# Query, key and value products as three 16-bit products of halves, with the splitting work dealt anew to the engines

## The reference

```
mod = silu(c) @ wmod                      # sa, ca, ga, sb, cb, gb for each batch
h   = layernorm(x) * (1 + ca) + sa
q, k, v = split(h @ w_qkv)                # 256 -> 3 * 256, 16 heads of 16
q, k = elu(rope(q) * s) + 1, elu(rope(k) * s) + 1
out[t] = q[t] . sum(k v, up to t) / max(q[t] . sum(k, up to t), 1e-6)   # causal linear attention
x   = x + ga * (out @ w_out)
h   = layernorm(x) * (1 + cb) + sb
x   = x + gb * (mixture of 8 experts of width 1024, top 2 of a softmax router)(h)
```

## Time and profile before

| | us |
|---|---|
| median of 3 runs (779.16 to 779.76) | 779.57 |
| span of the profiled execution | 776.0 |
| busy in the span: PE / DVE / ACT / POOL | 714.8 / 628.2 / 571.2 / 518.5 |
| steady part of the first phase, one chunk | about 9.5 |

### The profile page before, as it was taken

One profiled execution on the slowest core, in us unless ns is written; L12 is line 12 of the kernel. 1 busy time (PEld: TensorE's weight loads), 2 busy tenths in 40 slices (PEclk: granted clock), 3 DMA queues, 4 the chain that ended last, 5 costly groups with the idle time before them and its releaser, 6 DMA issues.

```text
span 776.0 us, 24871 instructions
## 1 busy us (share of the span) xinstructions
PE 714.8 (92%) x8105; PEld 549.7 (71%) x8105; DVE 628.2 (81%) x1494; ACT 571.2 (74%) x1108; POOL 518.5 (67%) x535
## 2 busy tenths in 40 slices
PE   8799999999999999845799999999999999999994
PEld 5467777777777776634677777777777777777772
DVE  4999999999999888778577777777777777777773
ACT  2799899999999998740476767777776767677772
POOL 5777777777777776547466666666666666666642
PEclk9999999999999999855799999999999999999997
DMA  6324344444443412310343343344333333443410
GB/s 226 113 67 133 110 135 120 131 120 139 124 140 116 151 64 67 120 48 8 96 77 69 71 73 74 76 70 79 70 75 69 77 69 76 76 72 76 72 21 1
DMA packets 52854, 69.27 MB, mean 89 GB/s; under 512 B 8864, under 2 KB 44080, under 8 KB 52736
## 3 DMA queue, kind: packets, MB, share of 16 engines
q0 software_dynamic: 18176, 27.06, 18.6%
q1 hardware_dynamic: 34560, 40.61, 16.9%
HBM read 46.50 MB, written 22.05 MB: 88 GB/s over the span
## 4 chain that ended last, share of the span: by engine, by line
PE 51%; DVE 2%; POOL 2%; issue 1%; DMA 1%; ACT 0%; POOLq 0%; DVEq 0%; ACTq 0%
PE hidden L1457 16%; PE bank L1475 15%; PE hidden L1459 8%; PE bank L1477 8%; PE bank L1292 2%; POOL mod_b L960 1%; PE bank L1309 0%; DMA xt<-ffn_rows,gi 0%; DMA out_dram<-x,si 0%; DVE stage L651 0%; PE bank L1300 0%; PE bank L1389 0%; POOL out_dram L1008 0%; DVE feat L652 0%; POOL mod_b L962 0%
## 5 line engine op out<-in xcount | busy, mean ns | idle before, releaser
L1457 PE MATMUL hidden<-qstT,w1hi_k 128*128 128x256 f16 x1136 | 197.9, 274 | 0.7 <-DVE qstT L755 0.7
L1459 PE MATMUL hidden<-qstT,w1lo_k 128*128 128x128 f16 x1136 | 193.6, 220 | 0.0
L1475 PE MATMUL bank<-w,amhi 128*128 x568 | 188.4, 379 | 0.1
L1477 PE MATMUL bank<-w,amlo 128*128 x568 | 154.8, 273 | 0.0
L1008 POOL DMA_INDIRECT out_dram<-x,si x71 | 115.2, 1622 | 38.8 <-issue 25.8
L791 DVE TENSOR_TENSOR amlo<-am,amhi 128x512 f16<-128x512 f32 x142 | 98.3, 693 | 49.2 <-ACT am L1168 49.2
L1457 PEld LDWEIGHTS hidden<-qstT,w1hi_k 128*128 x1136 | 111.7, 98 | 14.0 <-issue 1.1
L1459 PEld LDWEIGHTS hidden<-qstT,w1lo_k 128*128 x1136 | 111.6, 98 | 0.2
L1309 PE MATMUL bank<-wq,hT 128*128 128x512 f32 (+1 forms) x256 | 98.8, 511 | 1.3 <-DVE hT L524 1.2
L1475 PEld LDWEIGHTS bank<-w,amhi 128*128 128x128 f16 x568 | 55.6, 98 | 59.9 <-issue 0.4
L1167 ACT ACTIVATE amhi<-am 128x512 f16<-128x512 f32 x142 | 88.1, 620 | 0.3 <-DVE am L785 0.3
(11 more groups left out here) (219 smaller groups left out, 1783.6 us busy)
## 6 DMA issues: line engine op xcount, KB each, us to landing
stage<-in_L_ffn_w_dram SPq DMA_DIRECT2D x32, 512.0 KB, 4.3
xt<-in_L_attn_x_dram SPq DMA_DIRECT2D x32, 128.0 KB, 4.0
out_dram<-x SPq DMA_DIRECT2D x32, 128.0 KB, 3.7
ffn_rows<-h SPq DMA_DIRECT2D x32, 128.0 KB, 1.8
ffn_rows<-am SPq DMA_DIRECT2D x32, 128.0 KB, 4.2
am<-mod_rows SPq DMA_DIRECT2D x16, 128.0 KB, 4.0
mod_b<-mod_rows SPq DMA_DIRECT2D x8, 256.0 KB, 4.4
w<-in_L_wmod_dram SPq DMA_DIRECT2D x6, 256.0 KB, 4.6
```

Of the source, the lines that this page charges most:

```text
L1457: t.matmul(dst.rearrange("p (q n) -> p q n", q=2), w1s[0][k][g][:, w_], both, start=(k == 0), stop=False)
L1459: last = t.matmul(dst[:, P:2 * P], w1s[1][k][g][:, w_], both[:, 0, :], start=False, stop=(k == KT - 1))
L1475: t.matmul(y[:, :], ghi[:, m.p, c_m], w2s[mt // 2][:, bass.ds(w_, 2 * D)], start=(mt == 0), stop=False)
L1477: last = t.matmul(y[:, D:2 * D], glo[:, m.p, c_m], w2s[mt // 2][:, bass.ds(w_, D)], start=False, stop=(mt == MT - 1))
```

## The change

- From chunk 3 on (`PLAIN = 3`) `qk` and `v` are three 16-bit products per contraction step (high x high, high x low, low x high). Chunks 0 to 2 still take the 32-bit products, straight from the staged weights `wq_raw`.
- New steps: `wqh` (ACT, twice 128 x 768, once) and `wql` (DVE, twice 128 x 768, once) split the weights, scaled by 64. `hh` (ACT, 128 x 256) and `hl` (POOL, 128 x 256) split `hT`. `hT` and `h16` have one buffer each, and `v` and `qk` wait for `hl`.
- `hTe` moves from DVE to ACT (`Identity` with scale and bias from tensors). `whi` moves from ACT to POOL (two `tensor_scalar`).
- `slo` becomes one POOL instruction of 128 x 512 for q and k together; the slots of low x low hold zeros.
- `vhi`, `vlo` and the first three `rope`s take a factor of 64 into account; instruction counts of `vlo` stay, `rope` of chunks 0 to 2 has three instructions, not two.
- All orders are new. On DVE `den`, `rec`, `at` (now lag 4) stand around `ve` and ahead of `nb`, and `f` follows `nb`. On POOL `rs` is followed by `whi`. The closing of DVE no longer ends with `wlo`.

```diff
-ORDER_DVE = (("st2", 5), ("st", 0), ("mv2", 5), ("mv", 0), ("ve", 0), ("f", 2), ("sl0", 3), ("nb", 0), ("rope", 1),
-             ("stl", 3), ("x1", 4), ("hTe", 0), ("sl1", 3), ("wlo", 1), ("vlo", 0), ("den", 3), ("rec", 3), ("at", 3))
-ORDER_POOL = (("rs", 0), ("shk", 2), ("slo", 2), ("wb", 4), ("R", 1), ("xm2", 5), ("h2", 5))
-ORDER_ACT = (("exp", 2), ("sh0", 3), ("shq", 2), ("sth", 3), ("aTe", 4), ("xn", 0), ("sh1", 3), ("whi", 1),
-             ("kTs", 2), ("xn2", 5), ("vhi", 0), ("h2Te", 6), ("qTs", 2), ("lge", 6))
+ORDER_PE = (("aT", 4), ("state", 3), ("ear", 3), ("hT", 0), ("sc1", 3), ("pj", 4), ("Tk", 2), ("h2T", 6), ("pv0", 3),
+    ("v", 0), ("Tq", 2), ("lg", 6), ("pv1", 3), ("sc0", 2), ("qk", 0))
+ORDER_DVE = (("st", 0), ("mv2", 5), ("mv", 0), ("den", 4), ("ve", 0), ("rec", 4), ("at", 4), ("nb", 0), ("f", 2),
+    ("sl0", 3), ("rope", 1), ("stl", 3), ("x1", 4), ("sl1", 3), ("wlo", 1), ("vlo", 0), ("st2", 4))
+ORDER_POOL = (("h2", 7), ("rs", 1), ("whi", 2), ("wb", 5), ("shk", 3), ("slo", 3), ("hl", 1), ("R", 2), ("xm2", 6))
+ORDER_ACT = (("lge", 7), ("exp", 2), ("sh0", 3), ("xn", 0), ("aTe", 4), ("shq", 2), ("sth", 3), ("hTe", 0),
+    ("hh", 0), ("sh1", 3), ("kTs", 2), ("xn2", 5), ("h2Te", 6), ("vhi", 0), ("qTs", 2))
-OPENING_PE = {0: (("hT", 0), ("qk", 0), ("v", 0)), 1: (("hT", 0), ("mod1", 0), ("v", 0), ("qk", 0))}
+OPENING_PE = {0: (("hT", 0), ("v", 0), ("qk", 0)),
+OPENING_ACT = {0: (("xn", 0), ("hh", 0), ("wqh", 0), ("hTe", 0)),
...
-                g.tensor_tensor(qst[:, :, 1:4:2, :], f[:, 0].broadcast_to([P, NH, 2, HD]), qst[:, :, 0:3:2, :],
-                                ALU.subtract)
-                g.tensor_tensor(kst[:, :, 2:4, :], f[:, 1].broadcast_to([P, NH, 2, HD]), kst[:, :, 0:2, :],
-                                ALU.subtract).then_inc(a_["slo"], 1)
+                g.tensor_tensor(lows, feat[:, :].rearrange("p (q h d) -> p q h d", q=2, h=NH), highs, ALU.subtract)\
+                    .then_inc(a_["slo"], 1)
+            def h_low16(m):
...
+                wait(pool, a_["hh"], m.n - PLAIN + 1)
+                g.tensor_tensor(h16[:, 1, :], hT[:, :], h16[:, 0, :], ALU.subtract).then_inc(a_["hl"], 1)
+            def weights_high(m):
+                wait(pool, s_w[m.p], 16 * (m.pairs + 1))
+                g.tensor_scalar(piece(m, 0, 0), staged(m, 0), WS, None, ALU.mult)
+                g.tensor_scalar(piece(m, 0, 1), staged(m, 1), WS, None, ALU.mult).then_inc(a_["whi"], 1)
...
+            def h_modulated(m):
...
+                for k in range(KT):
+                    last = v.activation(hT[:, k * P:(k + 1) * P], bank[0][:, k * P:(k + 1) * P], ACT.Identity,
+                                        bias=mod_t[:, bass.ds(k * B + m.b, 1)],
+                                        scale=mod_t[:, bass.ds((KT + k) * B + m.b, 1)])
...
+            def product16(dst, m, lo):
+
+                for k in range(KT):
+                    hi_, lo_ = (h16[:, c, k * P:(k + 1) * P] for c in range(2))
+                    last = mm3(dst, hi_, lo_, wq16[:, k, 0, lo], wq16[:, k, 1, lo], start=(k == 0), stop=(k == KT - 1))
+                return last
```

More of the change, by code:

```diff
@@ new lines @@
+OPENING_DVE = {0: (("st", 0), ("mv", 0), ("ve", 0), ("nb", 0)),
+    1: (("st", 0), ("mv", 0), ("ve", 0), ("nb", 0), ("vlo", 1), ("rope", 1), ("vlo", 0), ("wql", 1), ("wlo", 1)),
+    2: (("st", 0), ("sl1", 3), ("mv", 0), ("sl0", 3), ("ve", 0), ("stl", 3), ("nb", 0), ("rec", 3), ("mv2", 5), ("f", 2), ("rope", 1), ("x1", 4), ("wlo", 1), ("vlo", 0), ("at", 3), ("wql", 1), ("st2", 5), ("den", 3))}
+OPENING_ACT = {0: (("xn", 0), ("hh", 0), ("wqh", 0), ("hTe", 0)),
+    1: (("hh", 0), ("vhi", 1), ("xn", 0), ("hTe", 0), ("vhi", 0), ("rows", 0))}
@@ L222, in adaln_block @@
         v16 = sb("v16", [P, CPB, 2, NH, VW], F16)
-        qst = sb("qst", [P, NH, 4, HD], F16)
-        kst = sb("kst", [P, NH, 4, HD], F16)
+        stacks = sb("stacks", [P, 2 * STACK + 3 * HD], F16)
+        qst, kst = (stacks[:, q * STACK:(q + 1) * STACK].rearrange("p (h c d) -> p h c d", h=NH, c=4) for q in range(2))
+        by_stack = stacks[:, 0:2 * STACK].rearrange("p (q h c) -> p q h c", q=2, c=4 * HD)
+        highs, nothing = by_stack[:, :, :, 0:HD], by_stack[:, :, :, 3 * HD:4 * HD]
+        lows = stacks[:, HD:2 * STACK + 3 * HD].rearrange("p (q n) -> p q n", q=2)[:, :, 0:STACK].rearrange(
+            "p q (h c) -> p q h c", c=4 * HD)[:, :, :, 0:HD]
         qstT = sb("qstT", [P, 8 * P], F16)
@@ L293, in adaln_block @@
         wmod_raw = [[late(w2s[(k * 3 + j) // 4], (k * 3 + j) % 4 * 512, 512) for j in range(3)] for k in range(KT)]
+        wq_raw = [late(w1s[0][0][k], 0, 3 * D) for k in range(KT)]
         rw_raw = late(w2s[2], 1280, D, E)
@@ L514, in first_modulation @@
                     link(v.tensor_scalar(mod_t[:, n_], bank[1][:, n_], add, None, ALU.add))
-            def h_modulated(m):
-                wait(dve, a_["hT"], m.n + 1)
-                wait(dve, a_["qk"], m.n - 1)
-                wait(dve, a_["v"], m.n - 1)
-                if isinstance(m.n, int) and m.n == 0:
-                    first_modulation()
-                for k in range(KT):
-                    last = v.tensor_scalar(hT[:, m.p, k * P:(k + 1) * P], bank[0][:, k * P:(k + 1) * P],
-                                           mod_t[:, bass.ds((KT + k) * B + m.b, 1)], mod_t[:, bass.ds(k * B + m.b, 1)],
-                                           ALU.mult, ALU.add)
-                last.then_inc(a_["hTe"], 1)
+                marks["mod_t"] = link.n
             def v_low(m):
                 wait(dve, a_["vhi"], m.n + 1)
-                v.tensor_tensor(v16[:, m.c, 1, :, 0:HD], bank[2][:, 0:D].rearrange("p (h d) -> p h d", d=HD),
-                                v16[:, m.c, 0, :, 0:HD], ALU.subtract).then_inc(a_["vlo"], 1)
+                v.scalar_tensor_tensor(out=v16[:, m.c, 1, :, 0:HD], in0=bank[2][:, 0:D].rearrange("p (h d) -> p h d", d=HD),
+                                       scalar=1.0 if m.n < PLAIN else 1.0 / WS, in1=v16[:, m.c, 0, :, 0:HD],
+                                       op0=ALU.mult, op1=ALU.subtract).then_inc(a_["vlo"], 1)
             def rope(m):
@@ L543, in rope @@
                 qk = bank[1][:, :].rearrange("p (h o d) -> p h o d", o=2, d=half_d)
+                if m.n < PLAIN:
+                    v.scalar_tensor_tensor(out=ra[:, :].rearrange("p (h d) -> p h d", d=half_d),
+                                           in0=bank[1][:, :].rearrange("p (h d) -> p h d", d=half_d), scalar=WS,
+                                           in1=cos_t[:, m.c:m.c + 1, :].broadcast_to([P, 4 * NH, half_d]),
+                                           op0=ALU.mult, op1=ALU.mult)
+                    for o in range(2):
+                        last = v.scalar_tensor_tensor(
+                            out=rb[:, :].rearrange("p (h o d) -> p h o d", o=2, d=half_d)[:, :, o, :],
+                            in0=qk[:, :, 1 - o, :], scalar=WS,
+                            in1=sin_t[:, m.c, o:o + 1, :].broadcast_to([P, 2 * NH, half_d]), op0=ALU.mult, op1=ALU.mult)
+                    last.then_inc(a_["rope"], 1)
+                    return
                 v.tensor_tensor(ra[:, :].rearrange("p (h d) -> p h d", d=half_d),
@@ L593, in residual @@
                 wait(dve, a_["pj"], m.n + 1)
+                wait(dve, a_["xn2"], m.n - 1)
                 wait(dve, s_out[m.p], 16 * m.pairs)
@@ L834, in sum_constants @@
                 link(g.memset(state[:, :, :, :], 0.0))
+                link(g.memset(nothing, 0.0))
                 for t in (ones, upto):
@@ L1045, in earlier_done, with h_high @@
                     wait(act, a_["ear"], (CPB - 1) * prev.b + prev.c)
+            def h_modulated(m):
+                wait(act, a_["hT"], m.n + 1)
+                if m.n > PLAIN:
+                    wait(act, a_["hl"], m.n - PLAIN)
+                else:
+                    wait(act, a_["qk"], m.n)
+                    wait(act, a_["v"], m.n)
+                if m.n == 0:
+                    act.wait_ge(s_dve, marks["mod_t"])
+                for k in range(KT):
+                    last = v.activation(hT[:, k * P:(k + 1) * P], bank[0][:, k * P:(k + 1) * P], ACT.Identity,
+                                        bias=mod_t[:, bass.ds(k * B + m.b, 1)],
+                                        scale=mod_t[:, bass.ds((KT + k) * B + m.b, 1)])
+                last.then_inc(a_["hTe"], 1)
+            def h_high(m):
+                if m.n < PLAIN:
+                    return
+                wait(act, a_["hTe"], m.n + 1)
+                wait(act, a_["qk"], m.n)
+                wait(act, a_["v"], m.n)
+                copy(h16[:, 0, :], hT[:, :]).then_inc(a_["hh"], 1)
             def v_high(m):
@@ L1320, in v_product @@
                 wait(pe, a_["hTe"], m.n + 1)
+                wait(pe, a_["hl"], m.n - PLAIN + 1)
                 if isinstance(m.n, int) and m.n == 0:
```

104 lines of the change are left out of this document (64 added, 40 removed), and 70 rows, old and new, of tables (CLOSING_ACT, CLOSING_DVE, CLOSING_PE, CLOSING_POOL).

## The result

| | us |
|---|---|
| before, median of 4 runs on the same chip (779.16 to 779.93) | 779.66 |
| after, median of 4 runs (826.36 to 829.67) | 827.6 |
| ratio, with its 95% interval | 1.0619 (1.0605 to 1.0633) |
| span of the profiled execution, before / after | 776.0 / 825.3 |

The forecast was 772.5 with a range of 765 to 793. It was wrong in sign and in size, so what follows is a search for 49.3 us of span.

The account below looks back on a forecast made before the run. DVE was taken as the bound, PE and ACT close behind. 25 chunks at 9.31 - 9.54 = -0.23 give -5.8; closing -1.3 - 1.5 and opening +1.5 make -7.1, so 779.6 becomes 772.5 us, range 765 to 793.

Parts of the forecast that it names:

- I take 0.605, since the scaling has one input like the CAST.: POOL, each of two `whi` scalings per chunk: cost taken from the CAST of the same shape, 0.605 us; upper bound 1.163.
- the forecast of 9.31: Steady chunk length: DVE's ring of 8.91 plus 0.40 us of hold on `nb`, against 9.54 before.
- The ring: DVE's closed cycle per chunk through `nb`, which waits for POOL's `rs`: 8.73 - 0.63 + 0.81 = 8.91 us before holds.
- `nb` is held 0.4 us: DVE's `nb` runs beside POOL's `whi`, which starts directly behind `rs`: held 0.4 us a chunk, 0.96 at the other end.
- DVE is held at more places: Slower rival: `wlo` and `f` on DVE also held by POOL, ring 9.91, 787.6 us; chance 0.36, shared with dear `whi`.
- the decision point of 0.63: Total hold on DVE per chunk, 9.54 - 8.91 = 0.63 us, from which the slower rival decides.
- A sum without any hold would give 768.9 for the median: Whole kernel: median claimed if no DVE instruction is held by POOL, 768.9 us.
- the first rival: ACT alone sets the chunk at 9.15 us because `nb` slips in ahead of `whi`: 768.5 us, chance 0.16.
- I take +1.5 (0 to 3): Opening, chunk 0: ACT's weight splitting delays `hTe` (+0.7) and `v` goes ahead of `qk` (+1.0); taken as +1.5 us.
- The +1.0 for `v` ahead of `qk`: Opening, chunk 0 on PE: `v` (1.1 us) goes ahead of `qk`, which rotation waits for, +1.0 us.
- -1.3: Closing: the last `wlo`, 1.29 us between the last `nb` and the routing, is now done earlier, -1.3 us.
- -1.5: Closing: the last four chunks' PE products are shorter by 0.8 us each; half taken, -1.5 us (0 to -3).

Follow-up runs that it names:

- copies: The kernel after with POOL's two weight scalings (`whi`) replaced by plain copies, so the factor 64 is missing: 803.23 us, ratio 1.0259.
- two-input products: The kernel after with POOL's two scalings replaced by tensor-by-tensor products with a constant column of 64: 821.75 us, ratio 1.0497.
- copies and hook: The kernel after with plain copies for POOL's two scalings and POOL's once-only gated-weights work one step later: 796.18 us, ratio 1.0122.
- the copies behind `R`: The kernel after with plain copies for the scalings, moved behind `R`, `wlo` and weight loads one chunk later, gated-weights hook one step later: 823.5 us, ratio 1.056.
- both of those runs: The kernel after with copies behind `R`, `wlo` and loads one chunk later, hook one step later: 823.5 us; the same with `qk` first in chunk 0: 822.91 us.

## Why the prediction was wrong

**"I take 0.605, since the scaling has one input like the CAST."** This step failed first. The scaling took 1.50 us, and the upper bound, 1.163, was too low as well. I had bounded the cost by shape and by the number of inputs, and both were the wrong guide: the same product takes 1.04 us as a two-input instruction. The groups of POOL in the kernel before had a warning that I passed over, in the routing:

```profile
L960 POOL TENSOR_SCALAR mod_b<-blocks,feat 128x72 f32<-128x72 f16 x8 | 10.1, 1263 | 0.8
L964 POOL TENSOR_SCALAR wq<-wq 128x72 f32<-128x72 f32 x1 | 0.4, 393 | 0.1
L963 POOL TENSOR_TENSOR wq<-mod_b 128x72 f32<-128x72 f32 x1 | 0.3, 336 | 0.1
L950 POOL TENSOR_SCALAR stage<-stage 128x32 f32<-128x32 f32 x1 | 0.3, 288 | 0.1
```

The first takes its scalar from a tensor and is a comparison, so it isn't the same case. L964 and L950 have an immediate, as the scaling has. L964 is already dearer than the two-input row of its shape, and from L950 to L964 a column costs (393 - 288) / 40 = 2.6 ns. Carried on to 512 columns that is 0.393 + 440 x 0.0026 = 1.55 us; with the other row of 128 x 32 (322 ns) it is 1.17. This is an estimate over a long way, from 32-bit outputs, but its range holds the measured 1.50.

With 1.50 the sum of POOL would have been 7.44 - 1.16 + 0.95 + 2.98 = 10.2 us, which by itself ends the forecast of 9.31. Measured are 9.47. Of the difference 0.28 is `hl`, which took 0.67 in place of 0.95, and 0.33 is `rs`, which took 0.72 where it had taken 1.05 beside DVE's `f`.

**"The ring is 8.73 - 0.63 + 0.81 = 8.91 us", "`nb` is held 0.4 us".** The ring is right. The 0.4 is right as a number and partly by luck: it was worked out as the rest of a POOL instruction of 0.60, and the one that it met took 1.50. A hold to its end would have been near 1.3; it let `nb` go after 0.40. In four kernels the measured chunk is that ring and the holds that one chunk of their timelines shows:

| kernel | hold on `nb` | hold on `wlo` | 8.91 + holds | measured |
|---|---|---|---|---|
| after | 0.40 | 1.58 | 10.89 | 10.76 (10.99 in three of four) |
| copies | 0.38 | 0.54 | 9.83 | 9.82 |
| two-input products | 0.83 | 0.75 | 10.49 | 10.54 |
| copies and hook | 0.38 | 0.66 | 9.95 | 9.84 |

With the means of 60 to 260 us in place of one chunk (each `wlo` 1.385 us, so a pair of 2.68 as it is drawn) the kernel after comes to 8.91 + 0.40 + 1.40 = 10.71, against its average of 10.76. Where DVE has to wait for more than this ring, the sum falls short: 9.15 against 10.2 with `whi` on ACT, and 9.81 against 10.08 with the copies behind `R`.

**The rival "DVE is held at more places", 0.36.** This is the second step that failed, and the one that makes the chunk long: the sum put the hold on `wlo` at nothing, and it is 1.58 us. The rival named the place and the direction, and I had it outside of the sum. It was sized at 0.3 to 0.6 us, from what is left of a POOL instruction at a random moment. But the two orders repeat in each chunk, so the meeting isn't random: with `R` 1.3 us later behind `rs` than in the run with the copies, `wlo` meets `R` near its start and the modulation next, 1.58 us in every chunk. `f`, the other place that I named, is not held in the steady part. The total hold was 1.98 us, far over the decision point of 0.63; each kernel above this point is slower in its steady part, and none below it with DVE as the bound was run. The trace of the kernel before had shown the size, a little further in the timeline near 20 us that gave me the held `nb`:

```profile
22.30 2.74 DVE L607 SCALAR_TENSOR_TENSOR w1lo_k<-stage,w1hi_k 128x512 f16<-128x512 f32 x2
22.77 1.71 POOL L919 TENSOR_TENSOR ra<-ra,rb 128x512 f32<-128x512 f32 x1
```

There a pair of `wlo` takes 2.74 us beside POOL's low halves and `R`, held by 1.46, and `R` takes 1.71 in place of 1.27. "0.6 at worst" could have been read as 1.5 from it.

One figure beside the rivals is wrong in itself. "A sum without any hold would give 768.9 for the median": 768.9 is the profiled span of the sum with its hold. A ring of 8.91 gives 25 x -0.63 - 1.3 = -17.1, so 762.5, and with ACT's 9.15 as the floor 768.5, as in the first rival.

**The opening: "I take +1.5 (0 to 3)".** It was +16.1. Some 7 us are the hook, which I had not looked at: I listed what moves inside the steps and not what hangs between them. The rest I read from DVE's timelines; its parts weren't tried one by one. Up to `rs` of chunk 2 the kernel after is 4.96 us late. Of that 2.89 come from PE's first products: ACT's `hTe` ends at 11.64, as forecast (11.6), but I had set the products at full clock, and they ran at half of it. 0.87 is `wql`, which I had set at nothing, and 1.20 is `wlo`, which stood ahead of `vlo` in a wait before and now stands behind it. From there to the variance of chunk 3 another 3.5 us go, in the main because `f` waits 0.87 for ACT's `exp` and is held 0.45, `vlo` waits 1.15 for ACT's copy of `v`, and the second `wql` takes its 0.87.

```profile
25.97 1.13 DVE L578 SCALAR_TENSOR_TENSOR feat<-feat,rb 128x512 f32<-128x512 f32 x1 [0.87 <-ACT feat L1122]
28.50 3.01 DVE L639 SCALAR_TENSOR_TENSOR w1lo_k<-stage,w1hi_k 128x512 f16<-128x512 f32 x2
```

The pair of `wlo` takes 3.01 us here, but it took 2.74 before the change too, so little of the loss is its. The +1.0 for `v` ahead of `qk` was tried, in another order, and isn't there; PE's clock fell in both of those runs (0.81 from 11 to 14 us with `qk` ahead of `v`, 0.63 without).

**The closing.** "-1.3" for the `wlo` that no longer stands ahead of the routing fits the -1.1 from the last `rs` to the end, but the four runs of the kernel after lie 3.3 us apart, so this is not shown. "-1.5" for shorter products was wrong: +5.9 to the last `rs`. With the copies alone the same stretch is -1.1 and with the copies and the hook -0.7, so it is the scalings that the closing loses by, as in the steady part.

**PE and ACT.** The products came as worked out (six at 0.22 us, 151.19 to 152.28). PE as a whole came to 8.57 us and not to 8.0 to 8.3, and I have not traced the difference. With 8.57 and 8.78 us a chunk PE and ACT both have room, so what PE gains is off the path. ACT was judged right as a floor: with `whi` back on it the chunk is 10.2.

**What the change gives.** The products are cheaper on the one engine that was not the bound. The splitting that they need costs one instruction of ACT (`hh`, 0.42 us) and one of POOL (`hl`, 0.67) a chunk, and moving `hTe` off DVE drives `whi` to POOL, where it takes 1.50 us in place of 0.62. The new products alone, with `hTe` and `whi` left where they were, were not run, so what they would be worth by themselves is open.

## What to carry to other kernels

Price an instruction on POOL by rows with the same operation and the same kind of scalar, carried on by their cost per column, not by shape or the number of inputs alone. For a hold, ask the trace for the longest time that the same instruction has taken, not for its mean: here it was there, 2.74 us for a pair of 1.28. Where instructions of two engines hold each other, lay the two new lists side by side on one time axis and read off which instructions meet; the orders repeat, so a meeting costs its full length in each pass and not an average. Work that hangs between the steps of a pipeline has to be followed too when a list changes its lag.
